# A graph network on one core: constants read from PSUM, part rows loaded by twos, and sums that start from POOL's copy

## The reference, cut to what matters

```
x = LN(x + L0(x))   L0: (1+eps) x + segment_sum(relu(x[src] + edge_attr), dst)
x = LN(x + L1(x))   L1, twice: x = segment_sum(dinv[src]*dinv[dst] * x[dst], src)
x = LN(x + L2(x))   L2, twice: segment_sum(x[src], dst) @ w_rel + x @ w_root + b
x = LN(x + L3(x))   L3: relu(segment_sum(w_edge * (x @ w)[src], dst) + b)
```

## Time and profile before

| | us |
|---|---|
| median of 3 runs | 9735.9 (9727.46 to 9779.13) |
| profiled execution | 9638.26 |
| span of its trace | 9636.5 |
| rank stage (first to after the last L491) | about 2653 |
| select part of a plain pass (first L1219 to last L690) | about 583, four times |
| sum part of a plain pass | about 310, four times |

### The profile page before, as it was taken

The page is one execution under the profiler, slowest core; times in us unless marked ns, Lnnn a source line. Parts: engine busy times, 40 slices in busy tenths (PEclk is TensorE's granted clock), DMA queues, the critical chain, the costliest instruction groups (busy, mean ns, idle before and its releaser), DMA issues. The chain is left out here.

```text
span 9636.5 us, 224105 instructions
## 1 busy us (share of the span) xinstructions
PE 6840.5 (71%) x65909; PEld 5511.2 (57%) x65909; DVE 7111.9 (74%) x11423; ACT 4647.4 (48%) x13851; POOL 5750.1 (60%) x6132
## 2 busy tenths in 40 slices
PE   9877776767772177799566866685678766867777
PEld 8755554545551166799445744573457545766666
DVE  6655565555554577799877977797779677979997
ACT  0345454544442266644676067506740675069920
POOL 0387787777784066533465556564555465648874
PEclk9855555555555555555666966796679667955588
DMA  9465666654235799744577977896789578936686
GB/s 340 102 176 166 163 175 175 172 157 114 73 75 176 253 306 302 230 122 122 182 270 280 355 243 269 290 350 212 266 293 339 189 270 284 357 132 231 230 305 233
DMA packets 1139377, 2162.48 MB, mean 224 GB/s; under 512 B 391662, under 2 KB 607726, under 8 KB 1138510
## 3 DMA queue, kind: packets, MB, share of 16 engines
q1 hardware_dynamic: 812062, 1231.35, 42.6%
q0 software_dynamic: 224928, 663.45, 18.1%
q10 hardware_dynamic: 101904, 261.43, 8.1%
HBM read 1227.26 MB, written 928.49 MB: 224 GB/s over the span
## 5 line engine op out<-in xcount | busy, mean ns | idle before, releaser
L522 POOL DMA_INDIRECT messages_in_parts<-WORK,goal x1850 | 1999.8, 1081 | 1194.2 <-ACT WORK L690 675.3
L491 POOL DMA_INDIRECT edge_rows<-WORK x1664 | 2101.5, 1263 | 907.9 <-issue 490.6
L923 PE MATMUL psum<-BIG,WORK 128*128 x11840 | 1586.7, 303 | 887.3 <-ACT WORK L690 480.6
L1219 DVE TENSOR_TENSOR WORK<-WORK,psum 128x1024 bf16<-128x1024 uint8 x1480 | 1707.8, 1215 | 621.0 <-remote 511.7
L690 ACT CAST WORK<-psum 128x432 bf16<-128x432 f32 (+1 forms) x4440 | 1765.4, 547 | 602.2 <-remote 390.6
L923 PEld LDWEIGHTS psum<-BIG,WORK 128*128 128x128 bf16 x11840 | 1129.0, 130 | 1344.5 <-issue 942.3
L541 POOL TENSOR_TENSOR BIG<-BIG,WORK 128x48 f32 x2220 | 1214.0, 547 | 972.9 <-ACT WORK L706 393.0
L1016 DVE TENSOR_TENSOR WORK<-lane_k,slot_part 128x1024 bf16<-128x1024 bf16 x2220 | 1548.3, 729 | 24.0 <-remote 13.1
L951 PE MATMUL psum<-WORK 128*128 128x144 bf16 x14800 | 1260.0, 235 | 332.6 <-DVE WORK L1016 273.2
L951 PEld LDWEIGHTS psum<-WORK 128*128 128x128 bf16 x14800 | 1099.7, 147 | 493.4 <-issue 385.4
L929 PE MATMUL psum<-BIG,WORK 128*128 x17760 | 984.3, 214 | 419.6 <-issue 248.1
(11 more groups left out here) (180 smaller groups left out, 10191.7 us busy)
## 6 DMA issues: line engine op xcount, KB each, us to landing
WORK<-messages_in_parts SPq DMA_DIRECT2D x1850, 288.0 KB, 4.5
WORK<-parts_by_slot SPq DMA_DIRECT2D x444, 640.0 KB
BIG<-edge_rows SPq DMA_DIRECT2D x148, 1040.0 KB
messages_in_parts<-BIG ACTq DMA_DIRECT2D x37, 2880.0 KB
WORK<-blocks_by_edge SPq DMA_DIRECT2D x416, 256.0 KB
edge_rows<-BIG ACTq DMA_DIRECT2D x1, 76960.0 KB, 242.8
BIG<-whole_messages SPq DMA_DIRECT2D x370, 193.5 KB, 2.4
whole_messages<-BIG ACTq DMA_DIRECT2D x37, 1920.0 KB
```

The lines of the kernel that those rows point to most:

```text
L491: pool.indirect_dma_start(rows_dram, bass.IndirectOffsetOnAxis(ap=at_stage[g][:, j:j + 1], axis=0), row_buf[g][:, j, :], None).then_inc(s_ ...
L522: pool.indirect_dma_start(unit_dram, bass.IndirectOffsetOnAxis(ap=goal[1 - d][:, t:t + 1], axis=0), msg[c].rearrange("p k f -> p (k f)"), ...
L923: m = pe.matmul(o, select[c % GB][:, k, :], V3[:, ds(b * W3, W3)], start=True, stop=True)
L1219: m = v.tensor_tensor(SEL[c % GB], part_row[c // GB][:, c % GB, :], here_p.to_broadcast([128, T * K]), ALU.is_equal)
```

## The change

Three edits.

1. `lane_rk`, a uint8 constant in SBUF, becomes `lane_p`, a float32 constant in PSUM bank 6 (396 words, unused in the rank stage). Both `equal` calls of `rank_onehots` read it.
2. The part rows lie in five buffers of PR = 2 rows instead of two of 5, ten rows as before, with a semaphore for each. SP issues five loads of 256 KB for ten batches instead of two of 640 KB; DVE waits at every second selector.
3. For the passes by source POOL copies H into AGG ahead of its adds (after the scatters of that pass and `s_whole`), so the clearing before them goes away and so does DVE's H+AGG. DVE's wait for `s_cleared` moves to POOL, for all passes. The squared norm is computed once, in q = 0, and q = 1 ends in one multiplication.

```diff
+PR = 2
-        lane_r = sb("lane_r", [128, NBX * RC], U8)
-        lane_rk = lane_r[:, :].rearrange("p (m c) -> p m c", c=RC)
-        part_row = [carve(128, [GB, T * K], U8) for _ in range(2)]
+        part_row = [carve(128, [PR, T * K], U8) for _ in range(RING // PR)]
+        lane_p = bank[6][:, 0:NBX * RC].rearrange("p (m c) -> p m c", c=RC)
-                def load_parts(i, s):
-                    sp.dma_start(part_row[s].rearrange("p a b -> p (a b)"),
-                                 part_dram[1 - d][ds(i * RING + s * GB, GB), :].rearrange("t n -> (t n)")
-                                 .unsqueeze(0).to_broadcast([P, GB * T * K])).then_inc(s_prow[s], 16)
+                def load_parts(i, j):
+                    sp.dma_start(part_row[j].rearrange("p a b -> p (a b)"),
+                                 part_dram[1 - d][ds(i * RING + j * PR, PR), :].rearrange("t n -> (t n)")
+                                 .unsqueeze(0).to_broadcast([P, PR * T * K])).then_inc(s_prow[j], 16)
                 def load_more(i):
-                    for s in range(2):
-                        sp.wait_ge(s_sel, i * RING + (s + 1) * GB + q * BATCHES)
+                    for j in range(RING // PR):
+                        sp.wait_ge(s_sel, i * RING + (j + 1) * PR + q * BATCHES)
                         sp.sem_inc(s_sp_turn, 1)
-                        load_parts(i + 1, s)
+                        load_parts(i + 1, j)
                         if kind == "edge":
-                            sp.wait_ge(s_z, i * RING + (s + 1) * GB)
-                            sp.sem_inc(s_sp_turn, 1)
-                            load_rows(i + 1, s)
+                            for s in range(2):
+                                if j * PR < (s + 1) * GB <= (j + 1) * PR:
+                                    sp.wait_ge(s_z, i * RING + (s + 1) * GB)
+                                    sp.sem_inc(s_sp_turn, 1)
+                                    load_rows(i + 1, s)
...
+                if d == SRC:
+                    pool.wait_ge(s_whole, q + 1)
+                    pool.tensor_copy(AGG, H).then_inc(s_cleared, 1)
+                wait_past(pool, s_cleared, q)
...
-                    pool.memset(AGG, 0.0).then_inc(s_cleared, 1)
+                    if PASSES[q + 1][0] == DST:
+                        pool.memset(AGG, 0.0).then_inc(s_cleared, 1)
...
-                    m = equal(oh[k][g % RS], lane_rk, blk[k][:, ds(n * RC, RC)])
+                    m = equal(oh[k][g % RS], lane_p, blk[k][:, ds(n * RC, RC)])
...
-            step(v.tensor_copy(lane_rk, lane_ck[:, :, 0:RC]))
+            step(v.tensor_copy(lane_p, lane_ck[:, :, 0:RC]))
...
-                    if c % GB == 0:
-                        dve.wait_ge(s_prow[c // GB], i * 16 + (q * PAIRS + 1) * 16)
+                    if c % PR == 0:
+                        dve.wait_ge(s_prow[c // PR], i * 16 + (q * PAIRS + 1) * 16)
...
-                wait_past(dve, s_cleared, q)
...
+                    step(v.tensor_tensor(stat[:, 3, :], dinv[:, :], dinv[:, :], ALU.mult))
                     step(v.tensor_tensor(H3, X3, per_node(dinv[:, :]), ALU.mult))
                 elif q in (1, 2):
 
-                    step(v.tensor_tensor(H, H, AGG, ALU.add))
+                    step(v.tensor_tensor(H3, A3, per_node(stat[:, 3, :] if q == 1 else dinv[:, :]), ALU.mult))
                     v.sem_inc(s_agg, 1)
-                    step(v.tensor_tensor(H3, H3, per_node(dinv[:, :]), ALU.mult))
-                    if q == 1:
-                        step(v.tensor_tensor(H3, H3, per_node(dinv[:, :]), ALU.mult))
-                    else:
+                    if q == 2:
```

More of the change, by code:

```diff
@@ L268, in gnn_program @@
         s_value = sem("node_values_ready")
-        s_prow = [sem(f"part_rows_loaded{s}") for s in range(2)]
+        s_prow = [sem(f"part_rows_loaded{s}") for s in range(RING // PR)]
         s_sel, s_spread = sem("selectors_ready"), sem("messages_selected")
@@ L437, in _ @@
                 wait_past(sp, s_sel, q * BATCHES)
-                for s in range(2):
-                    load_parts(0, s)
-                    if kind == "edge":
+                for j in range(RING // PR):
+                    load_parts(0, j)
+                if kind == "edge":
+                    for s in range(2):
                         load_rows(0, s)
@@ L1218, in selector @@
                     if kind == "plain":
-                        m = v.tensor_tensor(SEL[c % GB], part_row[c // GB][:, c % GB, :], here_p.to_broadcast([128, T * K]), ALU.is_equal)
+                        m = v.tensor_tensor(SEL[c % GB], part_row[c // PR][:, c % PR, :], here_p.to_broadcast([128, T * K]), ALU.is_equal)
                     else:
-                        m = v.tensor_scalar(SEL[c % GB], part_row[c // GB][:, c % GB, :], here[:, 0:1], None, ALU.is_equal)
+                        m = v.tensor_scalar(SEL[c % GB], part_row[c // PR][:, c % PR, :], here[:, 0:1], None, ALU.is_equal)
                     m.then_inc(s_sel, 1)
```

## The result

The changed kernel took 10050.24 us (median of 4 runs, 10039.67 to 10058.26) against 9731.68 us for the kernel before (9707.01 to 9779.13): a ratio of 1.0321, 95% interval 1.028 to 1.0361. It is slower by 319 us; the prediction said 656 us faster.

A forecast was written before the change was run, and what follows sets the result against it. It took POOL to bound the rank stage and load-caused stands to slow the plain select parts, where nothing is full. Terms -425 - 230 + 10 - 15 = -660 from 9736 gave 9080 us, range about 8830 to 9430.

The forecast's parts named there:

- What bounds the kernel: POOL sets the rank stage (2601 of 2653 us); nothing is full in plain select parts; DMA engines bound the edge pass.
- 2.41 us stands: Plain select parts: DVE stands 2.41 us about once in five batches, put down to the 640 KB part-row load.
- 150.1 us of the earlier trace: Rank stage: stoppages of the DVE, PE and ACT chain, 21 times in 1900 us, taken as its own.
- Edit 1, the duration: Rank stage: every scatter would take 0.96 us instead of 1.263 mean; the comparison itself keeps about 562 ns.
- Edit 1, "what is next on this stage": Rank stage: chain pace plus stoppages gives 5.35 us a group, 2226 us against 2653, so -425 us.
- chain of 4.88 us: Rank stage: DVE, PE and ACT's pace per group where nothing held it, against POOL's floor of 5.04 us.
- wider end, -120: Rank stage: edit 1's smallest gain, if the chain keeps half of SP's 430.6 us of waiting as latency, 6.1 us a group.
- Edit 2: Plain select parts: smaller loads shorten the stands, 583 to 525 us, -58 a pass, -230 in all; edge pass +10.
- The rival "the load is not the cause": Plain select parts: loads do not cause DVE's stands, so edit 2 gives 0; total 9306 us, chance 0.35.
- The rule of the Trainium skill: Part-row loads: roughly fixed 2 us per transfer favours large ones; edit 2 would cost 888 us if none overlapped.
- Edit 3: Sums: three DVE operations of 5.06 us go, one multiplication is added, POOL's copy (6 us) is covered: -15 us.
- a pause for each load: Plain passes: every load costs 2.41 us whatever its size, +1163 us in all, total 10469 us; chance 0.05.

The follow-up runs named there:

- e10: Kernel before plus a POOL memset of 1100 words behind every fourth scatter of the plain passes: 9503.07 us, ratio 0.9884.
- e16: Kernel before with edit 1 alone plus a POOL memset of 700 words behind every second rank-stage scatter: 9516.81 us, ratio 0.9905.
- e1_lanes: Kernel before with edit 1 alone (lanes in PSUM): 9907.43 us, ratio 1.0286, rank stage 2919 us.
- e4: Kernel before with edit 1 plus a 1100-word memset that POOL waits for after each group's four rank-stage scatters: 9839.86 us, ratio 1.0204.
- e8_rows_once: Kernel before, plain passes loading part rows in full only for the first ten batches, later loads 1 KB: 9703.46 us, ratio 0.999.
- e11_narrow: Kernel before, with plain-pass scatters writing 384 bytes of each message row instead of 2304: 9623.44 us, ratio 1.0007.
- e2_twos: Kernel before with edit 2 alone (part rows by twos): 9699.43 us, ratio 1.0067, plain parts 607 us.
- e18_short_gaps: Kernel before with edits 1 and 3 plus a 400-word POOL memset behind every second scatter in both stages: 9006.52 us, ratio 0.9946.

## Why the prediction was wrong, point by point

- **What bounds the kernel.** Right for both stages as far as it went: POOL sets the rank stage, nothing is full in the plain part. What was missed is that the 2.41 us stands of the earlier trace rows and the 150.1 us of the earlier trace rows are of one kind: pauses of POOL took away both (e10, e16), and the traces of set E have neither. The prediction noted beside the first that the last scatter had started 2.09 us before the end, as the load 2.94 us, and took the load. The edge pass has such stands too, 108.8 us, so it was not only bound by its DMA engines.
- **Edit 1, the duration.** Right: L494 0.966 us for 0.96 forecast, 1608 us busy for 1600, L1025 at its old duration.
- **Edit 1, "what is next on this stage".** This is the step that failed, with 307 + 427 = 734 us between forecast and result by the two traces (277 + 427 = 704 by e1_lanes within its set). It took PE's stoppages, 150.1 us, as fixed and laid them on a chain of 4.88 us. By its own form of sum the result follows from the right size: 674.7 us over the 1900 / 7.12 = 267 groups of the stretch is 2.5 us a group, 4.88 + 2.5 = 7.4, near the 2960 / 416 = 7.12 measured. The stoppages are not the chain's own. They depend on how densely POOL scatters, and edit 1 took away the hold of 1.2 us a group (e1, e4, e16). The prediction's wider end, -120, was a chain latency and not this.
- **Edit 2.** The cause was wrong: the stands do not come from loads (e8_rows_once) nor from bytes (e11_narrow). Forecast -58 a pass, measured +17 (e2_twos), outside the ends of -117 and 0 that I gave it. The rival "the load is not the cause" had 0.35, and was right on the cause; it put the price of the edit at 0. In the edge pass +10 was forecast; the stage has +17 in the changed kernel and nothing against its own set in e2_twos (670 among 667 to 672).
- **The rule of the Trainium skill** (page "SBUF — State Buffer", section "The DMA setup-cost knee") had the right sign for edit 2. The estimate made with it, 888 us, is far over the 62 us of e2_twos, so whatever fixed cost there is was nearly all overlapped here.
- **Edit 3.** In accord: -15 forecast, -26 measured with an interval of some 20 us to either side. The copy of 4.11 us, taken at 6, was covered.
- **Slower, by the wrong road.** The rival on that side was a pause for each load, at 10469. No rival let edit 1 itself lose, and so slower had only 0.05. Such a rival belonged there: edit 1 took from POOL the only hold it had in each group, and the prediction did not ask what that hold was doing.

## What to carry to other kernels

When a change frees an engine that held a neighbour up, look for what ran well in the shadow of that hold, and price its loss. A stand that ends "remote" has no named cause: list what ended shortly before it on every engine, and test two candidates before putting a gain on one. And where POOL's indirect DMAs and PE's results share a loop and such stands appear, try a pause of POOL after every two to four of them, and measure in more than one set of runs: in set E the same pauses only cost time.

## What the runs showed of the hardware

- In sets A to D, four or more scatters of 0.96 us in an unbroken run on POOL go with results of PE that DVE and ACT see late: 658.6 us of such stands of DVE in 1900 us in e1_lanes, 5.2 us each, and 6.5 us in all with a gap of 0.84 us after every second scatter. PE's matmuls start in time (L848 at 2703.28, L1095 at 2710.15 in the changed kernel); whether they end late or only their signals come late is not shown.
- Gaps by what they left, plain passes: 0.43 us after each scatter, 377.0 us of stands where a kernel of the same set has 646.4; 1.17 us after four, 50.5; 1.17 us after five, 242.1. Rank stage, 1000 to 2900: 1.17 us after four, 457.1; 2.0 us after four, none. Whether the length of the run or POOL's share of time off its scatters decides is not shown.
- The bytes of the scatters and the loads beside them don't matter: DMA share 0.78, 0.46 or 0.31, much the same stands. Nor does the granted clock: 0.50 in e1_lanes and 0.52 in e18_short_gaps, with the stands and without.
- One set of runs (E) had the kernel before 6 to 7% faster than all the others, and in its two traces the edge pass took 605 and 611 us for 661 to 680 elsewhere, without the stands that it has elsewhere. Another set with the same chip number, B, was the slowest of the five.
- A memset that POOL waits for costs about 1.0 us beyond its own duration (e4_lanes_pause); where POOL waits for it only a round later, the next scatter starts 0.17 us behind it (e16_lanes_two_gaps).
